# Key and query stores on ScalarE's DMA queue, and one burst of 48 products of probabilities and values per head group

## The chip, the cores and the metric

The kernel runs on one core of a Trainium2 chip. The metric is the device time of one execution in microseconds (us). A profiled execution also has a span, from its first to its last recorded instruction.

## What is computed

Eight batch elements, each with 224 queries (`x`, 224 x 512) and a context of 750 rows of 512. Cross attention with 16 heads of 32, then a small routed layer. All arithmetic is float32; `where` stands for the padding mask.

```python
q = (query @ w_q.T + b_q).reshape(B, T, H, D)
k = (key @ w_k.T + b_k).reshape(B, S, H, D)
v = (value @ w_v.T + b_v).reshape(B, S, H, D)
scores = jnp.einsum('bthd,bshd->bhts', q * SCALING, k) + attn_bias[None]
scores = jnp.where(key_padding_mask[:, None, None, :], NEG_INF, scores)
attn = jax.nn.softmax(scores, axis=-1)
out = jnp.einsum('bhts,bshd->bthd', attn, v).reshape(B, T, E)
return out @ out_proj_w.T + out_proj_b
```

Here `query` is the layer norm of `x`, and `key` and `value` are the context. The result is added to `x`; a layer norm, the distances to 32 prototypes, the two nearest of them and their rank-16 products give the second addition.

## The kernel before

Two functions hold the work: `weave` (L206 to L974) does the projections and the attention of all eight batch elements, `finish` (L977 to L1511) the output projection and the routed layer. The change touches `weave`.

**Units.** `weave` runs 256 units w, 32 for each batch element b (u is the unit within the batch element). A unit is one head and one chunk c of 112 queries; eight units (four heads times two chunks) make a head group, and four head groups a batch element. In unit w TensorE does: `turn(w, 0)`, three transposes of the exponentials into `prob_ps[0]` (L909); `score(w + 2)`, two matmuls of queries and keys (L896, L900), the second of which waits until VectorE's `add(w + 1)` is done (L899); `turn(w, 1)`, three more transposes. VectorE copies one half of the transposed probabilities to `probs_sb` (L731) and runs `add(w + 2)` (L721: score plus bias, and the row's minimum). ScalarE runs `exp(w + 1)` (L561) and then copies the other half (L570).

**Bursts.** In every fourth unit (u % 4 == 1) TensorE ends with `weigh` (L914): 24 products of probabilities and values, the four heads side by side in four groups of 32 columns, for the chunk whose probabilities were finished last. The trace holds two records for each product, so 48 to a burst. Every second burst is followed by `turn_sums` (L935). `probs_sb` has two buffers, one chunk of four heads each; `score_sb` has four.

**Projections of the next batch element.** Between these pieces TensorE works on the tiles of batch element b + 1, in `project_steps` (L837): 216 steps (one matmul each) in 16 tiles. In the order of `NEXT_TILES`: keys 0 to 3 (first half of the context), values 0 to 2, queries 0 and 1, keys 4 to 7 (second half), values 3 to 5. `step_shares` (L115) gives each unit its number of steps, and cuts them into three pieces (behind `turn(w, 0)`, behind the score, behind `turn(w, 1)`); units with a burst get 0 or 1. When a key tile is complete, ScalarE writes its high part to `k_hi` (L539, `high_tile`), VectorE the low part to `k_lo` (L643, `low_tile`), and SyncE stores both to DRAM (`store_tile`, L339, two DMAs at L346; for queries L352). From there SyncE loads them back in the layout of the scores (`load_keys`, L356: 6 or 7 DMAs, with u % 8 == 6). After batch element 0 there are two staging buffers for keys (`key_staging`, L137): tile i takes buffer i % 2, and `high_tile` of keys 7 first waits until the store of keys 5 has landed (L537). ScalarE runs its program in order, so behind that wait stand `copy` and the next `exp`.

**SyncE's order.** All these DMAs, and the loads of the context halves (L332), of `x` (L337) and the stores of the attention (L380), are issued by SyncE into one hardware queue (q1 in the profile), in the order that L418 to L445 write down: in iteration w first the stores of tiles that ended in unit w - 1, then the loads.

**GpSimd** splits the next context half into a high and a low part (L460, L462), and in the last batch element the three weight matrices of `finish` (L482, L485), which it loads through its own software queue (q0, L477).

Of the kernel before, what the change touches and what calls it, by code (L numbers as in the profile page):

```python
# [8 lines left out]
F32 = mybir.dt.float32  # L9
F32R = mybir.dt.float32r  # L10
# [70 lines left out]
NSC = 4  # L81
CHUNKS_AT = (1, 3, 4, 6, 7, 9, 11, 12, 14, 15, 17, 19)
# [71 lines left out]
class Shared:  # L154


    def __init__(self, nc, ctx):
# [7 lines left out]
        self.ctx_raw = sb("ctx_raw", [P, 2 * KT, HC])  # L165
        self.w_stage = cut(self.ctx_raw, 0, [P, KT, E])
        self.at_in = cut(self.ctx_raw, 0, [P, NG, T])
        self.x_res = cut(self.ctx_raw, TC * E, [TW, TC, E])
# [37 lines left out]
def weave(nc, x, ctx_t, bias, mask, w_in_t, b_in, bv, b_out, scratch, attn_t, w_dram, sh):  # L206


    with ExitStack() as ctx:
# [23 lines left out]
        probs_sb = [sb(f"probs_sb{p}", [P, HG * ST, TW]) for p in range(2)]  # L233
        w_stage = [cut(score_sb, 0, [P, KT, E])] + [cut(probs_sb[p], 0, [P, KT, E]) for p in range(2)]
        mask_u8 = sb("mask_u8", [B, S], U8)
        mask_f = cut(score_sb, KT * E, [B, 1, S])
        k_hi = [sb(f"k_hi{r}", [P, HC], F32R)[:, :] for r in range(2)]
        k_lo = [sb(f"k_lo{r}", [P, HC], F32R)[:, :] for r in range(2)]
# [88 lines left out]
        def _(eng):  # L327
# [3 lines left out]
            def load_half(b, f):  # L331
                eng.dma_start(ctx_raw[:, f * KT:(f + 1) * KT, :],  # L332
                              ctx_t[b, :, HALF_AT[f]:HALF_AT[f] + HC].rearrange("(k p) s -> p k s", p=P))\
                   .then_inc(ctx_loaded[f], 16)
# [3 lines left out]

            def store_tile(b, n):  # L339
                kind, i = tiles_of(b)[n]  # L340
                if kind == KEYS:
                    f, g = divmod(i, NG)
                    r, n = key_staging(b, i)
                    eng.wait_ge(k_ready, 2 * NG * b + i + 1)
                    for part, src in enumerate((k_hi, k_lo)):
                        eng.dma_start(scratch["k"][b, part, g * P:(g + 1) * P, SO[f]:SO[f] + SH[f]],  # L346
                                      src[r][:, 0:SH[f]].bitcast(F32)).then_inc(k_stored[r], 16)
                if kind == QUERIES:
                    r, n = query_staging(b, i)
                    eng.wait_ge(q_ready, 2 * b + i + 1)  # L350
                    for part, src in enumerate((q_hi, q_lo)):
# [1210 lines left out]
```

## Time and profile before

| | us |
|---|---|
| median of 3 runs | 933.97 |
| lowest and highest | 930.74, 935.41 |
| the profiled execution | 936.17 |
| its span | 934.5 |
| TensorE matmul busy | 875.6 (94%) |
| VectorE busy | 612.5 (66%) |
| ScalarE busy | 501.9 (54%) |
| GpSimd busy | 185.1 (20%) |

Busy times come from the hardware profiler on that one execution. A matmul's record has its full latency, and neighbours overlap, so a TensorE that shows 97% busy can still have room; what counts is the distance between starts. The startup (everything before unit 0) takes 53.3 us, batch elements 0 to 6 take 53.3 to 673.7, batch element 7 runs to 735.4 without projections beside it, and `finish` takes the rest.

### The profile page before, as it was taken

The page shows a single profiled execution, that of the slowest core. Times are in us where ns is not written, and L with a number is a line of the kernel's source. Part 1 is how long each engine was busy: PE and PEld are TensorE (multiplying, and loading weights), DVE is VectorE, ACT ScalarE, POOL GpSimd, SP SyncE. Part 2 cuts the span into 40 slices and gives each one's busy share as a digit, 9 for nine tenths or more (in the row PEclk, how much of TensorE's full clock was granted, in tenths as well). Part 3 has the DMA queues.
Part 4 walks back from the last instruction along what each step waited for, and adds up shares of the span by engine and source line. Part 5 has one row for each costly group of instructions (what it writes and reads, how often), then busy time and mean ns, then how long its engine had stood idle before and what let it go on. Part 6 is the DMA issues. An engine that isn't in the chain of part 4 may idle for free. (4 is left out here: it accounts for less than half of the span.)

```text
span 934.5 us, 20905 instructions
## 1 busy us (share of the span) xinstructions
PE 875.6 (94%) x8016; PEld 760.6 (81%) x8016; DVE 612.5 (66%) x1458; ACT 501.9 (54%) x1065; POOL 185.1 (20%) x240
## 2 busy tenths in 40 slices
PE   6999999999999999999999999999899669999996
PEld 6888978887888889888888897889777458878884
DVE  6576757676666766667676676766677465666663
ACT  5255646564655665555655565656577333444441
POOL 0040112120211201120112011210084212333300
PEclk9999999999999999999999999999999978999999
DMA  8977555665565456545545755475464211212101
GB/s 265 276 199 167 139 123 144 152 160 124 136 157 141 120 137 147 155 121 153 146 122 138 167 145 138 106 162 147 100 161 115 67 40 40 69 59 69 59 20 40
DMA packets 79450, 119.77 MB, mean 128 GB/s; under 512 B 8517, under 2 KB 58797, under 8 KB 79362
## 3 DMA queue, kind: packets, MB, share of 16 engines
q1 hardware_dynamic: 76866, 109.91, 46.3%
q0 software_dynamic: 2496, 8.65, 3.0%
q8 instruction: 59, 0.97, 0.5%
q14 instruction: 29, 0.24, 0.1%
HBM read 79.25 MB, written 39.28 MB: 127 GB/s over the span
## 5 line engine op out<-in xcount | busy, mean ns | idle before, releaser
L561 ACT ACTIVATE score_sb<-score_sb,neg_max 112x750 f32<-112x750 f32 x256 | 235.7, 921 | 83.2 <-DVE neg_max L721 82.7
L721 DVE CUSTOM_DVE_ANT_0 score_sb<-score_ps,neg_bias 112x750 f32<-112x750 f32 x256 | 239.4, 935 | 59.4 <-PE score_ps L900 57.8
L909 PE MATMUL prob_ps<-ident,score_sb 112*125 112x112 f32 x1536 | 253.5, 274 | 6.0 <-ACT score_sb L561 5.2
L909 PEld LDWEIGHTS prob_ps<-ident,score_sb 112*125 112x125 f32 x1536 | 228.9, 190 | 32.6 <-issue 8.5
L570 ACT ACTIVATE probs_sb<-prob_ps 125x336 f32<-125x336 f32 x256 | 114.6, 448 | 178.3 <-PE prob_ps L909 176.9
L731 DVE COPY probs_sb<-prob_ps 125x336 f32<-125x336 f32 x256 | 129.4, 505 | 111.0 <-PE prob_ps L909 108.9
L896 PE MATMUL score_ps<-k_st,q_st 97*112 97x512 f32 x256 | 107.9, 422 | 0.2 <-DMA q_st<-q_parts 0.2
L469 POOL COPY rsum_wide<-rsum 112x256 f32<-112x256 f32 x32 | 12.7, 397 | 442.2 <-DVE rsum L740 442.1
L855 PE MATMUL acc<-ctx_hi,w_hi 128*128 128x376 f32 (+1 forms) x256 | 92.0, 359 | 7.6 <-DVE ctx_lo L756 6.6
L855 PE MATMUL acc<-ctx_lo,w_hi 128*128 128x376 f32 (+1 forms) x256 | 93.0, 363 | 0.0
L855 PE MATMUL acc<-ctx_hi,w_lo 128*128 128x376 f32 (+1 forms) x256 | 90.0, 351 | 0.0
L900 PE MATMUL score_ps<-k_st,q_st 97*112 97x238 f32 x256 | 73.8, 288 | 15.0 <-DVE neg_max L721 14.5
L926 PE MATMUL out_ps<-probs_sb,v_sb 125*32 125x112 f32 x3072 | 86.9, 261 | 0.6 <-ACT probs_sb L570 0.6
L863 PE MATMUL acc<-w_hi,ctx_lo 128*125 128x512 f32 x192 | 82.7, 431 | 0.0
L863 PE MATMUL acc<-w_hi,ctx_hi 128*125 128x512 f32 x192 | 81.0, 422 | 0.0
L863 PE MATMUL acc<-w_lo,ctx_hi 128*125 128x512 f32 x192 | 79.9, 416 | 0.0
L926 PEld LDWEIGHTS out_ps<-probs_sb,v_sb 125*32 125x32 f32 x3072 | 71.5, 110 | 10.0 <-issue 4.2
L900 PEld LDWEIGHTS score_ps<-k_st,q_st 97*112 97x112 f32 x256 | 45.3, 177 | 32.0 <-DVE neg_max L721 28.3
L855 PEld LDWEIGHTS acc<-ctx_hi,w_hi 128*128 128x128 f32 x256 | 49.2, 192 | 11.3 <-issue 6.1
L643 DVE SCALAR_TENSOR_TENSOR k_lo<-acc,bias_col,k_hi 128x376 fp32r<-128x376 f32 (+1 forms) x60 | 36.0, 600 | 32.0 <-ACT k_hi L539 32.0
L462 POOL TENSOR_TENSOR ctx_lo<-ctx_raw,ctx_hi 128x376 fp32r<-128x376 f32 x56 | 55.7, 994 | 4.7
L855 PEld LDWEIGHTS acc<-ctx_lo,w_hi 128*128 128x128 f32 x256 | 49.4, 193 | 2.0
(162 smaller groups left out, 1507.5 us busy)
## 6 DMA issues: line engine op xcount, KB each, us to landing
k_st<-k_parts SPq DMA_DIRECT2D x96, 375.0 KB
q_st<-q_parts SPq DMA_DIRECT2D x96, 112.0 KB
ctx_raw<-in_ctx_t SPq DMA_DIRECT2D x14, 752.0 KB, 6.7
k_parts<-k_hi SPq DMA_DIRECT2D x30, 188.0 KB, 2.1
k_parts<-k_lo SPq DMA_DIRECT2D x30, 188.0 KB, 2.6
k_parts<-k_hi SPq DMA_DIRECT2D x30, 187.0 KB, 4.0
k_parts<-k_lo SPq DMA_DIRECT2D x30, 187.0 KB, 4.8
xb<-in_x SPq DMA_DIRECT2D x8, 448.0 KB, 4.1
```

Of the source, the lines that this page charges most:

```text
L462: eng.tensor_tensor(ctx_lo[f][:, k, :], src, ctx_hi[f][:, k, :].bitcast(F32), ALU.subtract)\
L561: nc.scalar.activation(scores[:, w % NSC, :], scores[:, w % NSC, :], ACT.Exp, bias=neg_max[:, w % UB:w % UB + 1], scale=-1.0, accum_out=su ...
L570: nc.scalar.activation(probs_sb[q % 2][0:SW, h * ST + BT:(h + 1) * ST, :], prob_ps[1][0:SW, 0:BT * TW].rearrange("p (s t) -> p s t", s=BT) ...
L643: nc.vector.scalar_tensor_tensor(k_lo[r][:, 0:SH[f]], src[:, 0:SH[f]], bias_col[:, NG + g:NG + g + 1], k_hi[r][:, 0:SH[f]].bitcast(F32), A ...
L721: nc.vector.tensor_tensor_reduce(out=scores[:, w % NSC, :], in0=score_ps[:, at:at + S], in1=neg_bias[:, w // HG % TC, :], scale=1.0, scala ...
L731: nc.vector.tensor_copy(probs_sb[q % 2][0:SW, h * ST:h * ST + BT, :], prob_ps[0][0:SW, 0:BT * TW].rearrange("p (s t) -> p s t", s=BT))\
L855: last = nc.tensor.matmul(acc[n % 2][:, 0:SH[f]], w_part[a][1][:, k, g * P:(g + 1) * P], ctx_part[c][f][:, k, K_AT[f]:K_AT[f] + SH[f]], st ...
L863: last = nc.tensor.matmul(acc[n % 2][0:SW, :], ctx_part[c][f][:, k, at:at + SW], w_part[a][2][:, k, :], start=(r == 0), stop=(m == end - 1))
L896: nc.tensor.matmul(score_ps[:, at + main[0]:at + main[1]], q_st[p][:, h, c * TW:(c + 1) * TW], k_st[p][:, h, main[0]:main[1]], start=True, ...
L900: nc.tensor.matmul(score_ps[:, at + mid[0]:at + mid[1]], q_st[p][:, h, c * TW:(c + 1) * TW], k_st[p][:, h, mid[0]:mid[1]], start=True, sto ...
L909: last = nc.tensor.transpose(prob_ps[j][0:SW, s * TW:(s + 1) * TW], scores[:, w % NSC, (BT * j + s) * SW:(BT * j + s + 1) * SW], ident[0:T ...
L926: last = nc.tensor.matmul(out_ps[h * D:(h + 1) * D, c * TW:(c + 1) * TW], v_sb[b % 2][0:SW, s, (g * HG + h) * D:(g * HG + h + 1) * D], pro ...
```

## The change

- `store_tile` moves from SyncE's program to ScalarE's. In iteration w it stands behind `copy(w)` and any piece-1 `high_tile`, for the tiles that ended in unit w - 1, and waits for VectorE's low part there. In the startup the store of tile n - 1 stands behind `high_tile(0, n)`.
- `weigh` takes both chunks of a head group: 48 products (96 records) in one burst with u % 8 == 1, and none with u % 8 == 5.
- `probs_sb` has three buffers, `score_sb` three instead of four. To find the room, `ctx_raw` holds one half of the context instead of two (each half is loaded later: at u = 10 and u = 28), the key staging moves to a tensor shared with `finish`, the second half of context 0 and the weights of `finish` are staged in `v_sb[0]`. The weights' loads move from batch element 6 (u = 12) to batch element 7 (u = 2), behind the last product that reads `v_sb[0]`, and their splits from u = 1..19 to u = 4..22.
- `step_shares` gives steps to all units but those with u % 8 == 1: the shares of u = 0 to 31 were 9 1 9 9 9 1 9 7 7 0 7 7 7 0 12 14 15 0 13 9 9 1 9 9 9 0 7 7 6 1 13 0 and are 8 0 9 8 8 9 7 6 7 0 6 6 6 9 13 12 13 0 10 9 8 8 9 8 6 0 6 7 6 6 6 0.

```diff
-NSC = 4
+NSC = 3
+NPB = 3
...
-    busy, burst, last = 1000, 1500, UB - 1
-    room = sum(cost) + last * busy + (last // 4) * burst
+    last = UB - 1
+    share = sum(cost) / len([u for u in range(last) if u % UG != 1])
...
-        given += max(0.0, room / last - busy - (burst if u % 4 == 1 else 0))
+        given += share if u % UG != 1 else 0.0
...
@@ block.sync
-            def store_tile(b, n):
...
-            for n in range(2):
-                store_tile(0, n)
...
+            eng.wait_ge(ctx_ready[0], KT * 2)
             load_half(1, 1)
...
-                for n in ended(b + 1, u - 1, 0, 1, 2):
-                    store_tile(b + 1, n)
                 if u % UG == 6 and w // UG + 2 < B * NG:
                     load_keys(w // UG + 2)
...
-                    if u == 2:
-                        eng.wait_ge(ctx_ready[0], KT * (b + 2))
+                    if u == 10:
+                        eng.wait_ge(ctx_ready[1], KT * (b + 2))
                         load_half(b + 2, 0)
-                    if u == 12:
-                        eng.wait_ge(ctx_ready[1], KT * (b + 2))
+                    if u == 28:
+                        eng.wait_ge(ctx_ready[0], KT * (b + 3))
                         load_half(b + 2, 1)
@@ block.gpsimd
-                if b == B - 2 and u == 12:
-                    for f in range(2):
-                        eng.wait_ge(ctx_ready[f], KT * B)
+                if b == B - 1 and u == 2:
+                    eng.wait_ge(weigh_done, NG * (B - 1))
                     for i in range(KT):
                         load_weights(i)
@@ block.scalar
+            def store_tile(b, n):
+                kind, i = tiles_of(b)[n]
+                if kind == KEYS:
+                    f, g = divmod(i, NG)
+                    r, n = key_staging(b, i)
+                    eng.wait_ge(k_ready, 2 * NG * b + i + 1)
+                    for part, src in enumerate((k_hi, k_lo)):
+                        nc.scalar.dma_start(scratch["k"][b, part, g * P:(g + 1) * P, SO[f]:SO[f] + SH[f]],
+                                      src[r][:, 0:SH[f]].bitcast(F32)).then_inc(k_stored[r], 16)
...
             def copy(w):
                 q, h = divmod(w, HG)
-                if h == 0 and q >= 2:
-                    eng.wait_ge(weigh_done, q - 1)
+                if h == 0 and q >= NPB:
+                    eng.wait_ge(weigh_done, (q - NPB) // TC + 1)
...
                 for n in ended(b + 1, u, 1):
                     high_tile(b + 1, n)
+                for n in ended(b + 1, u - 1, 0, 1, 2):
+                    store_tile(b + 1, n)
                 if u % UG == 2 and w > UG:
                     sums_out(w // UG - 1)
@@ block.tensor
-                for s, h in itertools.product(range(ST), range(HG)):
+                for c, s, h in itertools.product(range(TC), range(ST), range(HG)):
...
-                if u % 4 == 1 and w > 4:
-                    weigh(w // 4 - 1)
-                    if (w // 4 - 1) % TC == 1:
-                        turn_sums((w // 4 - 1) // TC)
+                if u % UG == 1 and w > UG:
+                    weigh(w // UG - 1)
+                    turn_sums(w // UG - 1)
```

Three places show how instructions move. The first is SyncE's queue in batch element 0, units 20 to 25, before (L346 are the stores of keys 4, 5, 6 and 7 of batch element 1, L366 to L373 the loads of `load_keys`):

```order
L346 DMA k_parts<-k_hi 128x374
L346 DMA k_parts<-k_lo 128x374
L366 DMA k_st<-mask_rows 1x4x750
L370 DMA k_st<-k_parts 32x4x750
L373 DMA q_st<-q_parts 32x4x224
L370 DMA k_st<-k_parts 32x4x750
L373 DMA q_st<-q_parts 32x4x224
L370 DMA k_st<-k_parts 32x4x750
L373 DMA q_st<-q_parts 32x4x224
L346 DMA k_parts<-k_hi 128x374
L346 DMA k_parts<-k_lo 128x374
```

The last two rows, the store of keys 5, stood behind seven loads in the same queue; in the change the loads stand there alone.

The second is ScalarE now, from u = 21 to 24 of batch element 0 (L515 is `high_tile`, here of keys 5, 6 and 7; L534 are the stores of keys 5 and 6; L554 is `exp`, L563 `copy`):

```order
L515 ACTIVATE key_parts<-acc,bias_col 128x374
L563 ACTIVATE probs_sb<-prob_ps 125x336
L554 ACTIVATE score_sb,sums<-score_sb,neg_max 112x750
L563 ACTIVATE probs_sb<-prob_ps 125x336
L534 DMA k_parts<-key_parts 128x374 x2
L554 ACTIVATE score_sb,sums<-score_sb,neg_max 112x750
L515 ACTIVATE key_parts<-acc,bias_col 128x374
L563 ACTIVATE probs_sb<-prob_ps 125x336
L534 DMA k_parts<-key_parts 128x374 x2
L554 ACTIVATE score_sb,sums<-score_sb,neg_max 112x750
L515 ACTIVATE key_parts<-acc,bias_col 128x374
L563 ACTIVATE probs_sb<-prob_ps 125x336
```

Each stored tile puts two DMA issues between a `copy` and the next `exp`. The store of keys 5 is issued behind `copy(22)`, and the `high_tile` of keys 7 asks for it behind `exp(25)`.

The third is TensorE at u = 25 of batch element 0 now (L922 is `weigh`, L931 `turn_sums`, L907 the transposes, L894 and L898 the score, L861 steps of a value tile):

```order
L907 MATMUL prob_ps<-ident,score_sb 125x112 x3
L894 MATMUL score_ps<-k_st,q_st 112x512
L898 MATMUL score_ps<-k_st,q_st 112x238
L907 MATMUL prob_ps<-ident,score_sb 125x112 x3
L922 MATMUL out_ps<-probs_sb,v_sb 32x112 x48
L931 MATMUL out_ps<-ident,rsum_wide 128x112 x2
L907 MATMUL prob_ps<-ident,score_sb 125x112 x3
L861 MATMUL acc<-w_lo,ctx_hi 125x512
```

Before, each burst was 24 products, and another 24 stood four units away. The rest of this stretch is the same work in the same order.

## Rows read from the trace of the kernel before

**Rows 1.** The page, part 1: busy time of each engine

```profile
PE 875.6 (94%) x8016; PEld 760.6 (81%) x8016; DVE 612.5 (66%) x1458; ACT 501.9 (54%) x1065; POOL 185.1 (20%) x240
```

**Rows 2.** Stretches by batch element (0, 1, 2, 7): length, busy, clock, DMA share, GB/s

```profile
53.30:140.80 87.50, 85.29 (x824) 75.95 (x823) 59.28 (x134) 51.46 (x113) 13.65 (x20) 0.98 0.61 154
140.80:230.30 89.50, 87.23 (x872) 77.19 (x873) 60.04 (x136) 52.08 (x114) 14.05 (x21) 0.98 0.57 141
230.30:318.40 88.10, 85.71 (x873) 75.96 (x873) 60.01 (x136) 52.24 (x115) 14.02 (x21) 1.00 0.57 143
...
673.70:735.40 61.70, 53.33 (x694) 42.84 (x694) 45.97 (x105) 44.98 (x100) 34.71 (x41) 1.00 0.51 128
```

**Rows 3.** Waits in 53.3 to 673.7: who for whom, us, times, longest

```profile
PEld score_ps L900 <- DVE neg_max L721: 23.9, 27, 2.2
ACT k_hi L539 <- DMA k_parts<-k_lo: 16.8, 7, 2.6
```

**Rows 4.** Timeline of ScalarE, 387 to 391 us: start, duration, [idle before, releaser]

```profile
387.08 0.19 ACT L561 ACTIVATION_READ_ACCUMULATOR score_sb<-score_sb,neg_max 112x1 f32 x1
389.68 0.57 ACT L539 ACTIVATE k_hi<-acc,bias_col 128x374 fp32r<-128x374 f32 x1 [2.41 <-DMA k_parts<-k_lo]
```

**Rows 5.** Timeline of SyncE's queue, 376 to 396 us

```profile
377.99 0.57 SPq L366 DMA_DIRECT2D k_st<-mask_rows  x1
...
381.97 0.43 SPq L346 DMA_DIRECT2D k_parts<-k_lo  x1
```

**Rows 6.** Timeline of TensorE behind that wait

```profile
391.80 0.49 PE L900 MATMUL score_ps<-k_st,q_st 97*112 97x238 f32 x1 [1.63 <-DVE neg_max L721]
392.08 0.64 PE L863 MATMUL acc<-w_hi,ctx_lo 128*125 128x512 f32 x1
```

**Rows 7.** The stretch behind it: the columns of rows 2

```profile
392.10:395.30 3.20, 3.20 (x12) 2.71 (x12) 2.33 (x7) 2.20 (x6) 0.00 (x0) 0.50 0.22 81
```

**Rows 8.** All key stores of L346: issue to landing

```profile
DMA to landing us min/median/max: 1.9/2.6/7.7
```

**Rows 9.** The stretch in which the loads of `load_keys` move

```profile
379.00:386.50 7.50, 7.50 (x51) 7.24 (x51) 5.60 (x15) 4.79 (x12) 2.15 (x4) 1.00 0.96 195
```

**Rows 10.** GpSimd's own queue (L477): all landings, and one beside SyncE's loads

```profile
DMA to landing us min/median/max: 2.8/4.5/8.2
...
ctx_raw<-in_fa_t POOLq DMA_DIRECT2D x1, 256.0 KB, 6.6
```

**Rows 11.** TensorE around a burst (timeline); the group of its products (page, part 5)

```profile
444.44 0.48 PE L909 MATMUL prob_ps<-ident,score_sb 112*125 112x112 f32 x3
444.85 1.36 PE L926 MATMUL out_ps<-probs_sb,v_sb 125*32 125x112 f32 x48
446.14 0.58 PE L909 MATMUL prob_ps<-ident,score_sb 112*125 112x112 f32 x3
...
L926 PE MATMUL out_ps<-probs_sb,v_sb 125*32 125x112 f32 x3072 | 86.9, 261 | 0.6 <-ACT probs_sb L570 0.6
```

**Rows 12.** Timeline of TensorE: u = 3 and u = 21 of batch element 4

```profile
417.05 0.60 PE L881 MATMUL out_ps<-ident,xb 112*128 112x112 f32 x4 [0.29 <-DVE attn L745]
...
466.05 0.36 PE L900 MATMUL score_ps<-k_st,q_st 97*112 97x238 f32 x1 [0.32 <-DVE neg_max L721]
```

**Rows 13.** Groups of ScalarE in 53.3 to 673.7: busy, mean ns

```profile
L561 ACT ACTIVATE score_sb<-score_sb,neg_max 112x750 f32<-112x750 f32 x224 | 206.2, 920 | 59.3 <-DVE neg_max L721 59.1
L570 ACT ACTIVATE probs_sb<-prob_ps 125x336 f32<-125x336 f32 x223 | 100.2, 449 | 171.0 <-PE prob_ps L909 169.7
...
L539 ACT ACTIVATE k_hi<-acc,bias_col 128x376 fp32r<-128x376 f32 (+1 forms) x56 | 31.6, 564 | 22.4 <-DMA k_parts<-k_lo 16.8 <-PE acc L855 5.1
```

**Rows 14.** Timeline of batch element 7: VectorE behind a burst

```profile
708.51 0.51 DVE L731 COPY probs_sb<-prob_ps 125x336 f32<-125x336 f32 x1 [1.22 <-PE prob_ps L909]
```

**Rows 15.** Timeline: the last weight split, and its first reader

```profile
708.04 1.27 POOL L485 TENSOR_TENSOR w_lo<-ctx_raw,w_hi 128x512 fp32r<-128x512 f32 x1
...
736.10 0.46 PE L1399 MATMUL big<-w_hi,at_hi 128*112 128x512 f32 x1 [1.94 <-PEq L209]
```

More of the change, by code:

```diff
@@ L80 @@
 BT = ST // 2
[L81 to L82 removed]
+NSC = 3
+NPB = 3
+CHUNKS_AT = (4, 6, 7, 9, 10, 12, 14, 15, 17, 18, 20, 22)
 MASKED = 2.0 ** 127
@@ L232, in weave @@
         scores = score_sb[0:TW, :, :]
-        probs_sb = [sb(f"probs_sb{p}", [P, HG * ST, TW]) for p in range(2)]
-        w_stage = [cut(score_sb, 0, [P, KT, E])] + [cut(probs_sb[p], 0, [P, KT, E]) for p in range(2)]
+        probs_sb = [sb(f"probs_sb{p}", [P, HG * ST, TW]) for p in range(NPB)]
+        w_stage = [cut(probs_sb[p], 0, [P, KT, E]) for p in (2, 0, 1)]
+        ctx_raw_b = cut(v_sb[0], 0, [P, KT, HC])
+        wf_stage = cut(v_sb[0], 0, [P, KT, E])
         mask_u8 = sb("mask_u8", [B, S], U8)
-        mask_f = cut(score_sb, KT * E, [B, 1, S])
-        k_hi = [sb(f"k_hi{r}", [P, HC], F32R)[:, :] for r in range(2)]
-        k_lo = [sb(f"k_lo{r}", [P, HC], F32R)[:, :] for r in range(2)]
+        mask_f = cut(score_sb, 0, [B, 1, S])
+        k_hi = [sh.k_parts[:, r, :].bitcast(F32R) for r in range(2)]
+        k_lo = [sh.k_parts[:, 2 + r, :].bitcast(F32R) for r in range(2)]
         k_hi += [cut(v_sb[1], 2 * j * HC, [P, 1, HC])[:, 0, :].bitcast(F32R) for j in range(2)]
@@ L337, in load_x @@
                 eng.dma_start(x_in[:, :, :], x[b].rearrange("(c t) e -> t c e", c=TC)).then_inc(x_loaded, 16)
-            def store_tile(b, n):
[L340 to L351, printed above, removed]
-                        eng.dma_start(scratch["q"][b, part, 2 * i * P:(2 * i + 2) * P, :]
-                                      .rearrange("(g p) t -> p g t", p=P),
-                                      src[r][:, :, :].bitcast(F32)).then_inc(q_stored[r], 16)
             def load_keys(n):
@@ L397, in _ @@
                 eng.dma_start(w_stage[2][:, k, :], w_in_t[k * P:(k + 1) * P, 2 * E:]).then_inc(wv_loaded[k], 16)
-            for n in range(2, NG):
-                store_tile(0, n)
             eng.dma_start(neg_bias[:, :, :], bias.rearrange("(c t) s -> t c s", c=TC)).then_inc(bias_loaded, 16)
-            for n in range(NG, 2 * NG):
-                store_tile(0, n)
             eng.wait_ge(ctx_ready[0], KT)
@@ L408, in _ @@
             eng.dma_start(scratch["mask"], mask_f[:, 0, :]).then_inc(mask_stored, 16)
-            for n in range(2 * NG, 2 * NG + 2):
-                store_tile(0, n)
             eng.wait_ge(mask_stored, 16)
@@ L521, in _ @@
                         load_weights(i + KT)
-                if b == B - 1 and u == 24:
+                if b == B - 1 and u == 25:
                     split_attended(eng, sh, sh.at_loaded, sh.xr_loaded, 1, 0, passed)
@@ L549, in high_tile @@
                                              bias=nbq[:, g:g + 1]).then_inc(q_hi_ready, 1)
+            def store_tile(b, n):
[7 more added lines that the diff above has]
+                                      src[r][:, 0:SH[f]].bitcast(F32)).then_inc(k_stored[r], 16)
+                if kind == QUERIES:
+                    r, n = query_staging(b, i)
+                    eng.wait_ge(q_ready, 2 * b + i + 1)
+                    for part, src in enumerate((q_hi, q_lo)):
+                        nc.scalar.dma_start(scratch["q"][b, part, 2 * i * P:(2 * i + 2) * P, :]
+                                      .rearrange("(g p) t -> p g t", p=P),
+                                      src[r][:, :, :].bitcast(F32)).then_inc(q_stored[r], 16)
             def high_x(b, c, src):
@@ L599, in _ @@
                 high_tile(0, n)
+                if n:
+                    store_tile(0, n - 1)
                 if n < 2:
@@ L616, in _ @@
             eng.wait_ge(wv_ready, KT)
+            eng.wait_ge(wq_ready, KT)
             exp(0)
```

54 lines of the change are left out of this document (26 added, 28 removed).

## The prediction

> **What bounds the kernel now.** I read the page first: TensorE is busy 94% of the span, the others far less [rows 1]. A busy TensorE has overlapping records, so the next view is the stretches by batch element [rows 2]. They do the same work from 1 on (872 or 873 matmuls) and yet take 89.5 to 89.6 us or 88.0 to 88.1, the longer ones at a granted clock of 0.98, the shorter at 1.00. Batch element 7, with no projections, is another regime: 61.7 us, paced by the round through VectorE, ScalarE and TensorE.
>
> The waits name what breaks TensorE's row [rows 3]: the second score matmul waits for VectorE's minimum, 27 times, up to 2.2 us; and ScalarE waits 7 times, once per batch element, for a key store (16.8 us in all). One such place, followed through: ScalarE ends an exp at 387.27 and idles 2.41 us until the store of keys 5 has landed [rows 4]. That store's second DMA was issued at 381.97, right behind seven loads issued from 377.99 on [rows 5], so it landed 7.7 us after its issue, the longest of all key stores, where the median is 2.6 [rows 8]. From 379.0 to 386.5 the queue was moving those loads, at 195 GB/s and 96% busy [rows 9]; the store stood behind them. ScalarE's wait holds back the low part, VectorE's next add and so the score: TensorE idles until 391.80 and then runs at half distance, 0.43 us between matmuls [rows 6]; the granted clock of 392.1 to 395.3 is 0.50, the lower level of 1.2 GHz instead of 2.4 [rows 7]. By then TensorE had stood still for 1.6 us. So one late store costs its stall and, in four of seven batch elements, the slow clock behind it.
>
> **The change, part by part** (against the profiled execution, 936.2 us; that is 2.2 above the median of 934.0, as much as one or two of the slow stretches).
>
> *The stall at u = 26.* TensorE's distance from the first to the second score matmul is there some 1.9 us over the 0.23 of an undisturbed unit (389.78 less latency to 391.80 [rows 6]). Seven of them: 13.3 us. The half clock: 89.6 less 88.05 is 1.55, and batch element 0 shows 0.98 too, so four times 1.55: 6.2 us [rows 2, 7].
>
> *What replaces it.* The store now goes into a queue of its own, so it starts beside the loads and not behind them. But the new step shares put keys 7 sooner behind keys 5: issue behind copy(22), wanted behind exp(25). Units of 2.4 to 2.55 us make that about 3.0 us from the second issue to the wish, where it was 5.3 (381.97 to 387.27 [rows 4, 5]). The trace has no store in a second hardware queue beside these loads. Bounds: it lands after 2.6 us, as alone [rows 8], and nothing is waited for; or after 7.7, as now, and ScalarE waits 4.7. Nearest row: GpSimd's queue, where 256 KB landed after 6.6 us beside SyncE's loads and after 2.8 undisturbed [rows 10], so sharing costs up to 3.8 us. I take half of that, since a packet of these stores is small (1.5 KB): 4.5 to 5 us, so ScalarE waits nearly 2. TensorE used to absorb 0.5 of ScalarE's 2.4; now it meets the wait at the second transposes of u = 25, with a burst right behind that lets the others catch up. I leave 0.7 us per batch element: 4.9 us stay. A stall of 0.6 us at u = 21 was followed by no slow clock, so I charge none.
>
> The Trainium skill, in "DMA: Bandwidth & Descriptors", section "Issuing engines are not separate DMA queues", speaks against the gain: DMAs of several engines share the same 16 DMA engines and a second issuer only saves sequencer time; by that the 13.3 and 6.2 us would stay. Its section "Queues, rings and completion order" says that each DMA engine goes round-robin between the queues packet by packet, which would let a small store pass a queue of loads; the landings of rows 10 fit that, since those 256 KB did not wait for the loads to end.
>
> *Merged bursts.* A burst without steps: the transposes start at 444.44 and would be followed after 0.31; the next matmul starts at 446.14, so a burst costs TensorE 1.39 us [rows 11]. Its record of 1.36 less one latency of 0.26 is 1.10 from first to last start, and with the step to a next group 1.16. A second 24 products behind the first therefore cost 1.16 instead of 1.39: 0.23 saved on entry and exit (0.19 to 0.27), 4 times in 7 batch elements: 6.5 us. The price is that four more units per batch element hold steps, each with switches between transposes and steps worth 0.04: 1.1 us.
>
> *The stall at u = 21.* There a unit with hardly any steps follows one in which VectorE had a key tile, so the score comes too soon: 0.32 idle, 0.58 over the normal distance [rows 12]. The unit now has 8 steps: 7 x 0.58 = 4.1 us go. The like of it at u = 17 and u = 0 (0.3 each) stay.
>
> *The transposes of x.* They wait at u = 3 for VectorE's attention output [rows 12], which waits for ScalarE's copy of the sums at u = 2. Keys 0 now end in piece 1 of u = 2, so their high part (0.56 [rows 13]) runs between copy(2) and that copy of the sums, instead of before copy(2): 7 x 0.5 = 3.5 us are added.
>
> *ScalarE's own work.* Ten stored tiles per batch element, two DMA issues each; on SyncE an issue takes 0.43 [rows 5], so 0.85 a tile. A unit with high part and store then needs 0.92 + 0.19 + 0.45 + 0.56 + 0.85, some 2.8 us less small overlaps [rows 4, 13], against units of 2.4 to 2.55. It is hidden because exp runs a unit ahead and such units do not follow each other more than twice: ScalarE idles 171 + 59 us in these seven stretches [rows 13] and needs 60 more. Cost 0; if that cover goes, the next exp is late (last rival). The third score buffer costs nothing: add(w + 2) asks for transposes of unit w - 1, which precede those of w that VectorE has already waited for. Nor do three probability buffers: copy(12) asks for the burst of u = 9.
>
> *Context halves and weights.* Halves are loaded at u = 10 and 28 and split some ten units later; hidden. The last weight split ended at 709.3 and is first read at 736.1 [rows 15]; it starts about 10 us later: hidden by the other 27.
>
> *Startup and batch element 7.* ScalarE waited 2.6 us for a store before the transposed x: I count 0.7 us won. In batch element 7 VectorE already idles 1.22 us behind a burst [rows 14]; a burst twice as long makes that more, but only once per eight units, and the last burst of 48 ends `weave`: 1 us lost.
>
> Sum: -13.3 - 6.2 + 4.9 - 6.5 + 1.1 - 4.1 + 3.5 - 0.7 + 1.0 = -20.3. So 936.2 - 20.3 = 915.9; I say **915 us**, 2.0% under the median.
>
> **Rivals.**
> 1. *The store lands as alone*, no residue, and the x transposes lose nothing: another 8.4 us, about 907. For it: small packets. Chance 0.15.
> 2. *The stall stays as large as it is*, with its slow clock: sharing 16 DMA engines that are 96% busy helps the store only as much as the shorter time to the wish takes away. Then only -6.5 + 1.1 - 4.1 + 3.5 + 0.3 is left: 930.5, within 0.5% of the median. By the Trainium skill's rule above it would be this. Chance 0.10.
> 3. *The store waits behind the loads although it has a queue of its own* (slower). It lands 7.7 us after issue, wanted after 3.0: ScalarE stalls 4.7, TensorE some 3.4 at u = 25 and 26, and the slow clock follows each time: 5.0 us per batch element, 35 instead of 19.5. That gives 936.2 + 15.5 - 5.7 = 946. It decides from a landing of about 7 us on. Against it: rows 10. Chance 0.08.
> 4. *ScalarE's issues are slow.* If a pair costs 2.5 us instead of 0.85, it outruns the idle time of its units and every stored tile delays an exp: some 0.5 us x 70 = 35, 950 us. It decides from about 1.5 us a pair. Chance 0.05.
>
> **How the numbers follow.** The forecast has 0.62. A measurement of this kernel can tell 0.5% (4.7 us) from no change. Faster: forecast and rival 1, 0.77, and a little of rival 2; same: most of rival 2; slower: rivals 3 and 4. The range of the forecast by its own unknowns (residue 0 to 1.9 per batch element, merge 0.19 to 0.27) is 909 to 924; rival 1 is mostly taken in below, and above I go to 927. Left out are rivals 3, 4 and part of 2.
>
> **What would show it.** In the new trace: key stores on a queue q10 or the like issued by ScalarE, with a median landing near 2.6 us and the longest under 6; ScalarE's wait before a high part 7 times under 2.2 us; stretches of batch elements 1 to 6 all within 0.3 us of each other near 86 us at a clock of 1.00; bursts of 96 records with some 2.5 us from transposes to transposes. Wrong would be: a landing of over 7 us, a clock of 0.5 inside `weave`, an exp that waits behind DMA issues, or units of batch element 7 over 16 us in eight.

## The result, and the profile after

The changed kernel took **939.42 us** (median of 20 runs, 933.7 to 947.4), the kernel before 934.85 in the same measurement (20 runs, 928.8 to 937.8). The ratio is 1.0061, its 95% interval 1.0041 to 1.008. The predicted 915 and its range were wrong; a little slower is what came.

The profiled execution took 943.16 us, its span 941.5. The page, parts 1 and 3:

```profile
PE 871.4 (93%) x8016; PEld 766.4 (81%) x8016; DVE 610.1 (65%) x1458; ACT 503.4 (53%) x1065; POOL 185.4 (20%) x240
...
q1 hardware_dynamic: 49730, 77.98, 35.2%
q10 hardware_dynamic: 27136, 31.93, 10.4%
```

TensorE has the same 8016 matmuls as in [rows 1] and 4 us less busy time. The stores have their queue, q10. The stretches by batch element, with the columns of [rows 2], and one short stretch of batch element 4:

```profile
55.20:140.10 84.90, 82.93 (x775) 75.18 (x775) 58.51 (x134) 51.59 (x112) 13.67 (x20) 0.98 0.58 150
140.10:229.00 88.90, 86.07 (x873) 77.56 (x873) 59.62 (x136) 52.31 (x115) 14.04 (x21) 0.98 0.57 141
...
318.40:406.60 88.20, 84.66 (x873) 75.89 (x873) 59.59 (x136) 52.32 (x115) 14.01 (x21) 1.00 0.56 143
406.60:495.90 89.30, 85.79 (x872) 77.22 (x873) 59.60 (x136) 52.31 (x114) 14.01 (x21) 0.98 0.57 141
...
676.30:736.90 60.60, 51.83 (x642) 42.90 (x643) 45.16 (x102) 43.87 (x98) 36.89 (x44) 0.97 0.62 155
477.60:481.00 3.40, 3.08 (x51) 2.89 (x55) 2.40 (x8) 2.63 (x6) 0.00 (x0) 0.50 0.40 137
```

They should have been near 86 us at a clock of 1.00. Only batch element 3 kept the clock (88.2 us). The waits of 55.2 to 673 us name the place:

```profile
PEld prob_ps L907 <- ACT probs_sb L563: 16.9, 7, 2.8
ACT key_parts L515 <- DMA k_parts<-key_parts: 16.6, 7, 2.8
PE prob_ps L907 <- ACT probs_sb L563: 14.6, 7, 2.5
```

ScalarE's wait for the store of keys 5 is as large as it was in [rows 3] (16.8 us, 7 times). It has only moved: TensorE now meets it at the second transposes of u = 25, in front of the burst of 96 records. Batch element 4 from three timelines. SyncE's loads:

```profile
467.34 0.59 SPq L352 DMA_DIRECT2D k_st<-mask_rows  x1
...
470.38 0.49 SPq L359 DMA_DIRECT2D q_st<-q_parts  x1
```

ScalarE, which issues the store of keys 5 (L534) at 469.25, wants its buffer at 474.15 and gets it at 476.95:

```profile
469.25 0.81 ACTq L534 DMA_DIRECT2D k_parts<-key_parts  x2
...
473.96 0.19 ACT L554 ACTIVATION_READ_ACCUMULATOR score_sb<-score_sb,neg_max 112x1 f32 x1
476.95 0.57 ACT L515 ACTIVATE key_parts<-acc,bias_col 128x374 fp32r<-128x374 f32 x1 [2.80 <-DMA k_parts<-key_parts]
```

TensorE, which stands still and then runs its long burst at the lower clock (the 0.50 above):

```profile
474.60 0.48 PE L907 MATMUL prob_ps<-ident,score_sb 112*125 112x112 f32 x3
...
477.92 0.97 PE L907 MATMUL prob_ps<-ident,score_sb 112*125 112x112 f32 x3 [2.50 <-ACT probs_sb L563]
478.82 3.54 PE L922 MATMUL out_ps<-probs_sb,v_sb 125*32 125x112 f32 x96
...
482.53 0.49 PE L907 MATMUL prob_ps<-ident,score_sb 112*125 112x112 f32 x3
```

Unit 25 lasts 7.9 us from 474.60 to 482.53. The units with the same work and no wait, 9 and 17, last 3.76. Measured this way in the trace, from the first transposes of a unit to those of the next, u = 25 takes 7.3, 7.5, 7.8, 6.0, 7.9, 7.9 and 7.9 us in batch elements 0 to 6: 52.2, or 25.9 over seven undisturbed ones. The gains that the prediction counted elsewhere are there and pay for it: batch elements 0 to 6 take 621.1 us instead of 620.4 together. Of the 7.0 us by which the two spans differ, 1.9 lie in the startup and 4.4 behind batch element 6.

The store's two DMAs landed 5.6 and 7.3 us after their issue:

```profile
DMA to landing us min/median/max: 5.6/6.5/7.3
```

So the first question for the experiments was why a store in a queue of its own lands as late as one behind seven loads [rows 8], and whether that landing is all that went wrong.

### The profile page after: what moved, and what is told of

It reads as the page before. It is cut to its first block and busy times, and to the rows that moved or that the text cites. A ratio compares the mean times of both kernels' runs of the same rounds, so it can differ in the third digit from the quotient of the medians.

```text
span 941.5 us, 20874 instructions
## 1 busy us (share of the span) xinstructions
PE 871.4 (93%) x8016; PEld 766.4 (81%) x8016; DVE 610.1 (65%) x1458; ACT 503.4 (53%) x1065; POOL 185.4 (20%) x240
## 3 DMA queue, kind: packets, MB, share of 16 engines
q10 hardware_dynamic: 27136, 31.93, 10.4%
## 5 line engine op out<-in xcount | busy, mean ns | idle before, releaser
L554 ACT ACTIVATE score_sb<-score_sb,neg_max 112x750 f32<-112x750 f32 x256 | 236.4, 924 | 90.2 <-DVE neg_max L719 82.4
L907 PE MATMUL prob_ps<-ident,score_sb 112*125 112x112 f32 x1536 | 250.6, 272 | 23.5 <-ACT probs_sb L563 14.6
L907 PEld LDWEIGHTS prob_ps<-ident,score_sb 112*125 112x125 f32 x1536 | 231.1, 189 | 46.2 <-ACT probs_sb L563 16.9
L563 ACT ACTIVATE probs_sb<-prob_ps 125x336 f32<-125x336 f32 x256 | 114.8, 448 | 180.6 <-PE prob_ps L907 178.6
L894 PE MATMUL score_ps<-k_st,q_st 97*112 97x512 f32 x256 | 106.0, 414 | 0.0
L922 PE MATMUL out_ps<-probs_sb,v_sb 125*32 125x112 f32 x3072 | 90.4, 278 | 1.9 <-issue 1.2
L853 PE MATMUL acc<-ctx_lo,w_hi 128*128 128x376 f32 (+1 forms) x256 | 91.1, 356 | 0.0
L922 PEld LDWEIGHTS out_ps<-probs_sb,v_sb 125*32 125x32 f32 x3072 | 82.0, 119 | 6.3 <-issue 3.3
L861 PE MATMUL acc<-w_lo,ctx_hi 128*125 128x512 f32 x192 | 82.7, 431 | 0.0
L861 PE MATMUL acc<-w_hi,ctx_hi 128*125 128x512 f32 x192 | 80.0, 416 | 0.0
L861 PE MATMUL acc<-w_hi,ctx_lo 128*125 128x512 f32 x192 | 77.4, 403 | 0.0
L898 PE MATMUL score_ps<-k_st,q_st 97*112 97x238 f32 x256 | 73.2, 286 | 1.6 <-DVE neg_max L719 1.3
L641 DVE SCALAR_TENSOR_TENSOR key_parts<-acc,bias_col,key_parts 128x376 fp32r<-128x376 f32 (+1 forms) x60 | 36.4, 606 | 47.1 <-ACT key_parts L515 47.1
L898 PEld LDWEIGHTS score_ps<-k_st,q_st 97*112 97x112 f32 x256 | 45.2, 177 | 17.7 <-DVE neg_max L719 12.6
L439 POOL TENSOR_TENSOR ctx_lo<-ctx_raw,ctx_hi 128x376 fp32r<-128x376 f32 x56 | 55.5, 992 | 4.7
L853 PEld LDWEIGHTS acc<-ctx_hi,w_lo 128*128 128x128 f32 x256 | 49.3, 192 | 2.0
```

Of the source, the lines that this page charges most:

```text
L439: eng.tensor_tensor(ctx_lo[f][:, k, :], src, ctx_hi[f][:, k, :].bitcast(F32), ALU.subtract)\
L554: nc.scalar.activation(scores[:, w % NSC, :], scores[:, w % NSC, :], ACT.Exp, bias=neg_max[:, w % UB:w % UB + 1], scale=-1.0, accum_out=su ...
L563: nc.scalar.activation(probs_sb[q % NPB][0:SW, h * ST + BT:(h + 1) * ST, :], prob_ps[1][0:SW, 0:BT * TW].rearrange("p (s t) -> p s t", s=B ...
L853: last = nc.tensor.matmul(acc[n % 2][:, 0:SH[f]], w_part[a][1][:, k, g * P:(g + 1) * P], ctx_part[c][f][:, k, K_AT[f]:K_AT[f] + SH[f]], st ...
L861: last = nc.tensor.matmul(acc[n % 2][0:SW, :], ctx_part[c][f][:, k, at:at + SW], w_part[a][2][:, k, :], start=(r == 0), stop=(m == end - 1))
L894: nc.tensor.matmul(score_ps[:, at + main[0]:at + main[1]], q_st[p][:, h, c * TW:(c + 1) * TW], k_st[p][:, h, main[0]:main[1]], start=True, ...
```

## The experiments

Each time is the median beside runs of the kernel before on the same chip (932.8, 933.5 and 933.7 us in the three groups). "Changed kernel" is the one with all parts of the change.

**Nobody waits for that store.** Keys 7 are staged in the idle query staging, so `high_tile` of keys 7 asks for the first queries' store, long landed, and not for that of keys 5. Once on the changed kernel, once on the kernel before.

```diff
-    return (i % NG, i // NG) if b == 0 else (i % 2, 2 + NG * (b - 1) + i // 2)
+    if b == 0:
+        return i % NG, i // NG
+    if i == 2 * NG - 1:
+        return 4, b - 1
+    return i % 2, 2 + (NG - i % 2) * (b - 1) + i // 2
...
+        k_hi += [q_hi[0].rearrange("p a b -> p (a b)")[:, 0:HC]]
+        k_lo += [q_lo[0].rearrange("p a b -> p (a b)")[:, 0:HC]]
```

> The changed kernel, with keys 7 staged in the idle query staging, so that its high part waits for nothing recent; all queues and the order of loads stay. Theory 1: the landing of keys 5 stays at 7 us or more, but nobody waits for it; unit 25 is 3.76 us, the time about 910 us, ratio 0.974. Theory 2: unit 25 stays long, above 930 us. If the half clock is caused by the long burst and not by the stall, granted clocks of 0.5 stay inside the batch elements, some 1.6 us each.

> The kernel before, with keys 7 staged in the idle query staging. Theory 1: the stall at unit 26 and its slow clock go, 915 us, ratio 0.979. Theory 2: some other wait on the same queue takes its place, 925 us or more.

Changed kernel: 916.59 us (ratio 0.9818, 0.9771 to 0.9864). Kernel before: 915.48 (0.9814, 0.9791 to 0.9837). Both stalls were that one wait. On the kernel before it cost 17 us by the medians and 19.4 in the traces, near the 19.5 of the prediction. The store of keys 5 itself still landed 5.9 to 7.3 us after its second issue on the changed kernel, and no granted clock of 0.50 is left in batch elements 0 to 6 of either: with no stall ahead of it, the long burst keeps the full clock. But the two kernels come out level, where the rest of the change had been counted at 5.7 us. The traces say where: batch elements 0 to 6 take 595.0 us instead of 601.0, but the startup takes 1.5 us more, and batch element 7 with `finish` 5.4 more. `finish` alone is no steady measure here: from the last transposes to the end, kernels with the same `finish` took from 201.4 to 205.8 us.

**The loads two units later.** SyncE calls `load_keys` with u % 8 == 0 instead of 6, on both kernels:

```diff
-                if u % UG == 6 and w // UG + 2 < B * NG:
-                    load_keys(w // UG + 2)
+                if u % UG == 0 and w and w // UG + 1 < B * NG:
+                    load_keys(w // UG + 1)
```

> The kernel before, with load_keys moved from u % 8 == 6 to the next u % 8 == 0; the stores stay in SyncE's queue. Theory 1: the stall of 1.9 us at unit 26 and the slow clock behind it go in all seven batch elements, 13.3 + 6.2 us, so 934.9 - 19.5 = 915 us, ratio 0.979, without a second queue. Theory 2 (one queue is too little, the stores need one of their own): the loads, later now, delay another store or the scores, 930 us or more.

> The changed kernel, with load_keys moved from u % 8 == 6 to the next u % 8 == 0, so that the store of keys 5 meets no loads. Theory 1 (the loss is the late landing of that store, and the slow clock behind it): the store lands in about 2.6 us, unit 25 of each batch element takes 3.76 us instead of 7.3 to 7.9, batch elements 1 to 6 take 85.2 us instead of 88.2 to 90.9, and the time is 939.4 - 29 = 910 us, ratio 0.974. Theory 2 (the long burst and ScalarE's DMA issues cost the time by themselves): unit 25 stays above 5 us or another unit grows, the time stays above 930.

Kernel before: 916.93 us (0.9834, 0.981 to 0.9858), as expected. Changed kernel: 937.14 (1.0053, 1.002 to 1.0085), a plain miss. Its timeline of SyncE shows why:

```profile
465.46 0.59 SPq L352 DMA_DIRECT2D k_st<-mask_rows  x1
```

Unit 22 of batch element 4 began at 465.3 in this kernel. In the changed kernel the first load went out at 467.34 and unit 22 began at 467.2. So the loads did not move. With the stores gone from its program, SyncE runs ahead and stands in front of the loads' own wait for the scores, wherever the call is written. That is the first thing the change did unseen: the stores, with their waits for the low parts, had been what paced SyncE.

**The loads released two scores later.** So the wait itself was changed, for all loads and then for those of a batch element's first head group alone:

```diff
-                    eng.wait_ge(score_ready, UG * (n - 1))
+                    eng.wait_ge(score_ready, UG * (n - 1) + 2)
...
+                    eng.wait_ge(score_ready, UG * (n - 1) + (2 if g == 0 else 0))
```

> The changed kernel with one number more: load_keys waits for two more scores (8(n-1)+2 instead of 8(n-1)) before it issues its seven DMAs. The earlier try moved these loads by two units in SyncE's program and had no effect on when they started: 465.46 us, as the score of unit 22 began, where the changed kernel issues them at 467.34 with unit 22 at 467.2. Since the stores have left SyncE's program, SyncE runs ahead and is released by the wait for the scores, wherever the call stands. Theory 1 (the store of keys 5 lands late because the packets of these loads go ahead of its own, though it has its own queue): now the loads start at u = 24, some 3 us behind the store, which lands under 4 us after issue; ScalarE does not wait in front of the high part of keys 7, u = 25 takes 3.8 us in every batch element, none of their bursts runs at half clock, and the time is about 915 (912 to 919). Theory 2 (the store is slow for what it is: small packets on ScalarE's queue, whatever moves beside it): the wait stays near 2.5 us per batch element and the time near 939.

938.29 us (1.0063, 1.0035 to 1.0091): the total is theory 2's, the trace is theory 1's. The store of keys 5 is now issued ahead of the loads (its second DMA at 471.8, the first load at 473.33) and lands after 2.6 us at most:

```profile
473.33 0.59 SPq L352 DMA_DIRECT2D k_st<-mask_rows  x1
```
```profile
DMA to landing us min/median/max: 2.2/2.4/2.6
```

No key tile waits any more, and u = 25 takes 3.76 us everywhere. In its place stands another row of the waits of 55 to 673 us:

```profile
PE acc L853 <- DVE q_lo L659: 14.7, 7, 3.0
...
ACT q_hi L524 <- DMA q_parts<-q_lo: 13.0, 7, 2.8
```

The loads of another head group, delayed as well, now lie beside the store of the queries, which has its own reader: the same collision, six units earlier. Units 19 and 20 took up to 6.2 and 4.4 us instead of 2.9 and 2.4. Hence the narrower edit:

> The changed kernel with the two more scores asked for only by the loads of a batch element's first head group (g == 0), which are the ones beside the store of keys 5. The try before this asked for them in front of all loads: there the wait for keys 5 was gone (u = 25 took 3.8 us everywhere), but the loads of another group then lay beside the store of the queries, and ScalarE waited up to 2.8 us for that one at u = 19. Theory 1 (whichever store lies behind the loads lands late, on a queue of its own too; one that is issued ahead of them lands after 2 to 3 us): now no store that is waited for lies beside loads, u = 19 takes 2.9 us and u = 25 3.8 us in every batch element, and the time is that of the kernel with the stores on SyncE plus ScalarE's issues, 911 to 918. Theory 3 (ScalarE's queue as such costs the difference between 911 and 939, by delays that the waits don't name): still over 925.

916.01 us (0.9807, 0.9772 to 0.9841). No store is waited for after the startup, u = 19 takes 2.9 and u = 25 3.8 us. With every store still on ScalarE's queue, moving seven loads by two units took 23 us off. Theory 3 falls.

**The store sooner on ScalarE.** `store_tile` in front of `copy(w)`:

```diff
+                for n in ended(b + 1, u - 1, 0, 1, 2):
+                    store_tile(b + 1, n)
                 if w < UNITS:
                     copy(w)
                 for n in ended(b + 1, u, 1):
                     high_tile(b + 1, n)
-                for n in ended(b + 1, u - 1, 0, 1, 2):
-                    store_tile(b + 1, n)
```

> The changed kernel with store_tile in front of copy(w) instead of behind it, so that ScalarE issues the store of keys 5 some 1.0 us sooner (its low part is ready at 468.1, the issue was at 469.25 in batch element 4), still 1 us behind the first of the seven loads. Theory 1 (the store's packets are held up until the loads have moved): it lands at the same moment as before, so issue to landing grows by what the issue gained, the wait of ScalarE stays 2.4 us or more per batch element, and the time stays within 3 us of 939. Theory 2 (the place of the issue on ScalarE is what makes it late): the landing moves by the 1.0 us too, the wait falls to some 1.6 us, and the time falls by 1 us or more in each of seven batch elements, to 932 or less.

923.42 us (0.9869, 0.9834 to 0.9904), on the side of theory 2, and by more than it expected. In batch element 4 the two DMAs landed 4.4 and 5.4 us after issue, where the changed kernel had 5.6 and 7.3, so an issue 1.0 us sooner, counted from the start of unit 22, brought the landing forward by 3.0 (1.1 to 3.5 over the seven batch elements). ScalarE waited once, 0.7 us. The price is that `copy` now stands behind the wait for the low part: units 17 and 21 take 6.4 us more in all (waits of ScalarE, 55 to 660 us):

```profile
ACT probs_sb L563 <- DVE key_parts L641: 31.1, 20, 1.6
...
ACT key_parts L515 <- DMA k_parts<-key_parts: 0.7, 1, 0.7
```

What a store issued beside the loads meets is seen in the packets of the two queues. The changed kernel, 471 to 473 and 473 to 475 us (queue: packets, MB, share of 16 engines):

```profile
q1 hardware_dynamic: 196, 0.39, 99.8%
q10 hardware_dynamic: 13, 0.02, 3.9%
```
```profile
q10 hardware_dynamic: 245, 0.33, 55.1%
q1 hardware_dynamic: 221, 0.30, 49.0%
```

And this kernel, 463 to 465 us:

```profile
q1 hardware_dynamic: 203, 0.36, 56.2%
q10 hardware_dynamic: 155, 0.22, 34.6%
```

The 13 against 196 is a late start and not a small share. In the changed kernel the first of the store's 288 packets started 2.7 us after its first issue (1.7 to 3.6 in the other batch elements), where an undisturbed store's starts after 0.8. Once its packets moved, q10, which also held the store of keys 6 by then, had 245 of the 466 packets of the next 2 us. In this kernel the first packet also started 2.6 us after the issue, but 3.7 us after it 155 packets had started, and 13 in the changed kernel (6 to 18 in its batch elements 2 to 6, some 127 in 0 and 1). So neither theory was right as it stood: the store is neither held until the loads have moved, nor simply delayed by its own issue. It starts late, and then shares about evenly. How late it lands depends steeply on how far the loads are ahead of it; why its first packets start so late is not settled by these runs.

**Stores back on SyncE.** All else of the change stays:

```diff
@@ block.sync
+            for n in range(2):
+                store_tile(0, n)
...
+                for n in ended(b + 1, u - 1, 0, 1, 2):
+                    store_tile(b + 1, n)
                 if u % UG == 6 and w // UG + 2 < B * NG:
                     load_keys(w // UG + 2)
@@ block.scalar
-                for n in ended(b + 1, u - 1, 0, 1, 2):
-                    store_tile(b + 1, n)
```

> The changed kernel with store_tile back on SyncE, at its old places in SyncE's program: the merged bursts, buffers and step shares stay, only the queue part is undone. If a store in SyncE's queue waits for the loads in front of it as it did before (first load issued to landing 387.3+2.4-378.0 = 11.7 us), keys 5 land at about 467.3+11.7 = 479.0 in batch element 4, against 476.95 on ScalarE's queue, and ScalarE waits some 4.9 us instead of 2.8: 2 us more in each of seven batch elements, so about 953 (948 to 958). Then the queue move gained something, and what made the stall worse is that the new step shares ask for the buffer 2.6 us sooner. If instead the queue move is what made it worse, this kernel is faster than the changed one: under 935.

**911.3 us** (0.9739, 0.9704 to 0.9774): the fastest kernel of the study, 42 us from what was expected. Undoing the queue part turns a loss into a gain of 2.6%. Timeline of SyncE, batch element 4:

```profile
453.40 0.80 SPq L349 DMA_DIRECT2D k_parts<-key_parts  x2
454.62 0.58 SPq L369 DMA_DIRECT2D k_st<-mask_rows  x1
...
457.63 0.43 SPq L376 DMA_DIRECT2D q_st<-q_parts  x1
```
```profile
DMA to landing us min/median/max: 1.9/2.5/3.1
```

The store of keys 5 stands *ahead* of the seven loads. With the new step shares keys 5 end in u = 21, so the store belongs to iteration 22, where SyncE's program has `store_tile` in front of `load_keys`. Before, they ended later, and the store came behind the loads [rows 5]. So the new shares, in the old order of SyncE's program, remove the collision (no run has them without the merged bursts); the expectation had taken the old order for granted. SyncE also waits for the low part first, so that the loads go out 2.2 us after the start of unit 22 (452.4) and not 0.2. The stretches of batch elements 3 to 5, at full clock:

```profile
307.30:392.00 84.70, 83.68 (x872) 75.97 (x872) 60.26 (x136) 52.45 (x114) 14.02 (x21) 1.00 0.59 148
392.00:476.90 84.90, 83.84 (x874) 76.02 (x873) 60.43 (x136) 52.44 (x115) 14.04 (x21) 1.00 0.59 149
476.90:561.70 84.80, 83.81 (x872) 76.00 (x873) 60.31 (x136) 52.46 (x114) 14.04 (x21) 1.00 0.59 148
```

**Only the order swapped.** That kernel again, with `load_keys` in front of `store_tile` in each iteration:

```diff
-                for n in ended(b + 1, u - 1, 0, 1, 2):
-                    store_tile(b + 1, n)
                 if u % UG == 6 and w // UG + 2 < B * NG:
                     load_keys(w // UG + 2)
+                for n in ended(b + 1, u - 1, 0, 1, 2):
+                    store_tile(b + 1, n)
```

> The changed kernel with all stores back on SyncE (911.3 us when it ran), but in each iteration load_keys in front of store_tile instead of behind it. With the new step shares keys 5 end in u = 21, so their store belongs to iteration 22, the same as the loads; only this order decides which goes first. Theory 1 (the order of issue decides, and the queue hardly): the store of keys 5 lies behind seven loads in one queue, lands some 7 to 8 us after its issue and 11 to 12 behind the first load, the high part of keys 7 waits 3 us or more, TensorE stalls at u = 25 with a burst at half clock in most batch elements, and the time goes from 911 to 938 or more, at least as slow as with the stores on ScalarE. Rival (SyncE's stores are quick for another reason, their issuing engine): it stays under 918.

958.08 us (1.026, 1.0225 to 1.0295). Same engine, same queue, same bursts, and 47 us more for two statements in the other order. The swap also takes the store's wait away from in front of the loads, which go out 0.2 us behind the start of unit 22 instead of 2.2; the 47 us are for both. SyncE's timeline, then ScalarE's:

```profile
479.76 0.57 SPq L369 DMA_DIRECT2D k_st<-mask_rows  x1
...
483.87 2.24 SPq L349 DMA_DIRECT2D k_parts<-key_parts  x4
```
```profile
490.99 0.57 ACT L542 ACTIVATE key_parts<-acc,bias_col 128x374 fp32r<-128x374 f32 x1 [4.56 <-DMA k_parts<-key_parts]
```

The landing comes 11.2 us behind the first load (479.76 to 490.99), ScalarE waits 4.6, and u = 25 takes 10.4 to 10.9 us. In the changed kernel the landing came 9.6 us behind the first load, and the time was 19 us less. That gain is the sooner issue: ScalarE sends the second DMA 2.3 us behind the first load, SyncE, which has seven loads to issue first, 4.6 us behind it. Counted from that issue the store took 7.3 us in its own queue and 6.6 behind the loads in theirs, so no gain of the queue as such is seen. Either way it is far from being ahead of them.

**The queue part alone, on the kernel before.** `store_tile` moves to ScalarE as in the change; bursts, buffers and shares stay.

> The kernel before with the queue part alone: store_tile on ScalarE behind copy(w), as in the change; bursts of 24, four score buffers, two probability buffers and the old step shares stay. Theory 1a (the queue helps by some 2 us, since the landing comes 9.6 us behind the first load instead of 11.7, and the old shares ask for the buffer 9.3 us behind it): ScalarE waits 0.3 us or less, nothing reaches TensorE, and the time is 916 to 920, as when nobody waits for that store. Theory 1b (the queue move does not help, and the issue behind copy(w) comes later than SyncE's did): the wait stays 2.4 us or grows, and the time is 933 or more.

937.28 us (median of ten, of which one took 1657.33; the ratio without that one is 1.0034, 1.0004 to 1.0065): theory 1b. ScalarE waited 13.4 us in all, where [rows 3] has 16.8. This wait has another make-up (timeline of ScalarE in batch element 4; L560 is `copy`, L512 `high_tile`, of keys 5 and 7, L531 the store of keys 5):

```profile
472.70 0.57 ACT L512 ACTIVATE k_hi<-acc,bias_col 128x374 fp32r<-128x374 f32 x1
...
476.55 0.45 ACT L560 ACTIVATE probs_sb<-prob_ps 125x336 f32<-125x336 f32 x1 [1.12 <-PE prob_ps L903]
476.64 0.33 ACTq L531 DMA_DIRECT2D k_parts<-k_hi  x1
...
477.00 0.46 ACTq L531 DMA_DIRECT2D k_parts<-k_lo  x1
...
482.65 0.57 ACT L512 ACTIVATE k_hi<-acc,bias_col 128x374 fp32r<-128x374 f32 x1 [1.60 <-DMA k_parts<-k_lo]
```

The high part of keys 5 is done at 473.27 and the low part at 474.90, but the store goes out only behind `copy(23)`, its second DMA at 477.00: 5.2 us behind the start of unit 22, where SyncE issued it 3.5 to 4.0 us behind in batch elements 1 to 6 of the kernel before. It lands 5.6 us later, 11.3 us behind the first load (471.35), where it had been 11.7. From its issue it lands sooner than the 7.7 us of [rows 8], but the later issue, 5.6 us behind the first load where the changed kernel has 2.3, takes nearly all of that away.

## Why the prediction was wrong

**Right: what bounded the kernel before.** It priced the stall at u = 26 and its slow clock at 19.5 us. With nobody waiting for keys 5 the kernel before takes 601.0 us for batch elements 0 to 6 instead of 620.4: 19.4.

**Right as a sum, partly by luck: the rest of the change.** It was -6.5 + 1.1 - 4.1 + 3.5 - 0.7 + 1.0 = -5.7. The kernel with stores on SyncE has it without the stall. Its span is 909.7, that of the kernel before with nobody waiting 914.7: -5.0. Term by term:
- A burst of 96 records takes 2.25 us from first to last start, where one of 48 took 1.10, so the second half costs 1.15, as predicted.
- Unit 21 goes from 3.12 to 2.44 us (0.58 predicted).
- Unit 3, with the transposes of x, goes from 3.44 to 3.65, so 0.2 and not 0.5 is lost.
- Batch element 7, up to its last unit, goes from 57.2 to 58.4 us, near the 1.0 that was counted. From there to the end it is 204.8 instead of 202.2, but that part scatters by over 4 us between traces of kernels with the same `finish`, so no cause is shown for the 2.6.
- Two interruptions of a burst cost 3.6 us and were not foreseen (below).
- The startup is 1.3 us shorter, though both of these kernels store from SyncE; the 0.7 of the prediction was for stores on ScalarE, with which the startup grew.

Misses of either sign offset each other, so the -5.0 is no check of each term.

**Wrong: "What replaces it".** The term was 4.9 us left of the stall; it measured 25.9. Three steps failed, of which the first had the landing and the other two the order wrong.
1. *"So it starts beside the loads and not behind them", landing after 4.5 to 5 us.* It lands after 7.3. The row for it was a transfer on GpSimd's queue [rows 10], whose 3.8 us of delay were halved "since a packet of these stores is small". Small packets did not help: the first of them started 2.7 us after the issue, 1.9 later than undisturbed, and only 13 had started after 3.7 us. That row, taken whole, would have given 2.6 + 3.8 = 6.4. The wish came 4.5 us after the second issue and not 3.0, which is why ScalarE waited 2.8 and not 4.7.
2. *The order was not traced to the end.* The order rows ahead of the prediction show that keys 5 are now stored in iteration 22. In SyncE's old program that is ahead of the loads. The prediction priced the queue as the cure of a collision that the new shares had already removed, and that the move of the queue brought back: on ScalarE the first issue stands 2.1 us behind the start of unit 22 (1.0 on SyncE), and the loads moved forward from 2.2 us behind it to 0.2.
3. *SyncE's waits were not seen as a brake.* Taking the stores out of its program also takes their waits out. What stands behind them starts sooner.

**Rival 3 came nearest**, with its chance of 0.08. It said that it decides from a landing of about 7 us, and so it did, though the store did not wait for the loads to end: it started late and then moved beside them. Its price of 5.0 us per batch element was 3.7, because the wish came later. The sum with 3.7 is 936.2 - 19.5 + 25.9 - 5.7 = 936.9. The profiled execution took 943.2: the startup grew by 1.9 us instead of shrinking by 0.7 (55.2 instead of 53.3; ScalarE's wait there for a landed store reads 3.8 us, 3.0 the longest), and batch element 7 with `finish` by 4.4 instead of 1.0. Rival 2 had the stall staying as large; it rested on the Trainium skill, "DMA: Bandwidth & Descriptors", section "Issuing engines are not separate DMA queues", by which a second issuing engine saves only the sequencer's time. The landing agrees with it: 7.3 us after the issue in a queue of its own, 6.6 in that of the loads. The rule on packet-wise turns in "Queues, rings and completion order", which the prediction set against it, fits the packets once both queues move (245 against 221); it does not give the late start, 13 packets against 196 in the 2 us before.

**Where the difference between 911.3 and 939.4 lies.** The profiled executions differ by 31.8 us (spans 909.7 and 941.5): 25.9 at u = 25, 2.2 in the startup, 1.7 in batch element 7, whose first burst ran at a clock of 0.50, 3.7 in small delays of the other units, 0.3 behind them. The broken bursts in batch elements 0 to 6, two with the stores on SyncE and one in the changed kernel, give back 2.0. The queue move itself, with the loads out of its way, costs 4.7 us against the kernel with stores on SyncE (916.0 to 911.3), half of it in the startup (first transposes at 55.5 instead of 53.0).

## What to carry to other kernels

Before moving a DMA to another engine's queue, write down what it stands ahead of and behind in the old one, *after* all other parts of the change are in. A transfer that somebody waits for should be issued ahead of bulk loads; an engine that need not issue them first got it out 2.3 us and landed 1.6 us sooner, still behind them; ahead of them it landed 4 us sooner after its issue. And a program that loses its waits runs ahead: look at what it then releases sooner. When a change has two parts that touch the same wait, time each alone; here the one without the other was worth 22 us, and the other took 28 away.

## What the hardware showed that was not expected

- **Beside bulk loads a store starts late and then shares about evenly.** In the changed kernel the first packet of keys 5 started 1.7 to 3.6 us after the issue, undisturbed after 0.8. Over 471 to 473 us it was 13 packets against 196, over 473 to 475 us 245 against 221.
- **A stall in front of a long burst is dear.** In six of seven batch elements the burst behind the wait ran at 0.50 (3.3 to 3.9 us instead of 2.25 from first to last start); before, the slow clock followed the stall in four of seven [rows 7].
- **A burst of 96 records can break in the middle.** With the stores on SyncE it happened at u = 1 of batch elements 1 and 2, where nothing was waited for (timeline of TensorE; L928 are the products):

```profile
137.87 1.74 PE L928 MATMUL out_ps<-probs_sb,v_sb 125*32 125x112 f32 x64
141.33 0.97 PE L928 MATMUL out_ps<-probs_sb,v_sb 125*32 125x112 f32 x32 [1.73 <-issue]
```

For 1.7 us the engine waited for nothing that the profile shows; the granted clock stayed 1.00. Seven of the eight kernels with the long burst show one or two such breaks, of 1.4 us or more from start to start, all at u = 1; no kernel with bursts of 48 records does. The cause was not tried.
